# A mixture-of-experts stage on one core: token transposes two experts ahead, and down products interleaved with gate products

## What is computed

```python
dispatch = dispatch.at[flat_e, pos_c].add(tokens[tidx] * valid[:, None])
g = jnp.einsum('ech,ehi->eci', dispatch, gate_w)
u = jnp.einsum('ech,ehi->eci', dispatch, up_w)
expert_out = jnp.einsum('eci,eih->ech', jax.nn.silu(g) * u, down_w)
...
output = jnp.zeros((t, h), tokens.dtype).at[tidx].add(contrib)
```

## Time and profile before

| what | value |
|---|---|
| median of three runs | 1327.19 us (1311.12 to 1372.49) |
| the profiled execution's own time | 1307.97 us |
| its span on the core | 1306.2 us |
| PE, busy share of the span | 98% |
| DVE | 70% |
| ACT | 50% |
| POOL | 33% |

### The profile page before, as it was taken

The page is one execution under the profiler, slowest core; times in us unless marked ns, Lnnn a source line. Parts: engine busy times, 40 slices in busy tenths (PEclk is TensorE's granted clock), DMA queues, the critical chain, the costliest instruction groups (busy, mean ns, idle before and its releaser), DMA issues.

```text
span 1306.2 us, 22561 instructions
## 1 busy us (share of the span) xinstructions
PE 1280.0 (98%) x7565; PEld 1123.8 (86%) x7565; DVE 916.0 (70%) x1787; ACT 647.3 (50%) x1053; POOL 433.9 (33%) x344
## 2 busy tenths in 40 slices
PE   6999999999999999999999999999999999999995
PEld 5888888888888888888889999999999999999994
DVE  7878877777777777785656667667766766676662
ACT  4421232212322123221256777777877777777772
POOL 1000000000000000000014666777666667676653
PEclk9999999999999999999999999999999999999998
DMA  7336554664546645445447999999999999999995
GB/s 269 121 107 163 130 121 127 157 166 98 130 119 153 167 104 131 114 118 134 134 133 214 286 278 286 287 290 292 290 291 285 298 291 287 282 295 285 298 277 65
DMA packets 203800, 263.65 MB, mean 202 GB/s; under 512 B 49268, under 2 KB 138744, under 8 KB 203768
## 3 DMA queue, kind: packets, MB, share of 16 engines
q1 hardware_dynamic: 175096, 191.93, 50.9%
q0 software_dynamic: 28672, 71.32, 23.7%
HBM read 178.18 MB, written 71.39 MB: 191 GB/s over the span
## 4 chain that ended last, share of the span: by engine, by line
PE 96%; DVE 2%; DMA 1%; ACT 0%; issue 0%; POOL 0%; SPq 0%; ACTq 0%
PE pmm L1255 18%; PE pmm L1257 18%; PE pmm L1256 18%; PE pout L1255 11%; PE pout L1257 11%; PE pout L1256 11%; PE ptr L1488 4%; PE plog L1316 2%; PE plog L1325 1%; PE ptr L1267 0%; DMA out_dram<-outs,slot_cols 0%; DVE stats L829 0%; DMA xbuf<-_L_attn_proj_matrix_dram 0%; DVE xt_lo L795 0%; PE plog L1345 0%
## 5 line engine op out<-in xcount | busy, mean ns | idle before, releaser
L1614 POOL DMA_INDIRECT out_dram<-outs,slot_cols x128 | 228.7, 1787 | 165.6 <-DMA out_dram<-outs,slot_cols 136.2
L1255 PE MATMUL pmm<-xt_hi,proj_hi 128*128 128x256 f32 (+1 forms) x784 | 253.0, 323 | 2.2 <-DVE xt_lo L795 1.4
L1257 PE MATMUL pmm<-xt_hi,proj_lo 128*128 128x256 f32 (+1 forms) x784 | 249.6, 318 | 0.0
L1256 PE MATMUL pmm<-xt_lo,proj_hi 128*128 128x256 f32 (+1 forms) x784 | 249.6, 318 | 0.0
L1255 PE MATMUL pmm<-xt_hi,sgu_hi 128*128 128x256 f32 (+1 forms) x768 | 246.1, 320 | 0.2 <-issue 0.2
L1256 PE MATMUL pmm<-xt_lo,sgu_hi 128*128 128x256 f32 (+1 forms) x768 | 243.4, 317 | 0.0
L1257 PE MATMUL pmm<-xt_hi,sgu_lo 128*128 128x256 f32 (+1 forms) x768 | 243.4, 317 | 0.0
L1598 POOL TENSOR_TENSOR earlier<-earlier,chosen 128x64 bf16<-128x64 bf16 x64 | 23.9, 373 | 617.8 <-DVE chosen L916 614.0
L1604 POOL DMA_INDIRECT xbuf<-rows,slot_cols x128 | 175.3, 1369 | 80.8 <-issue 38.6
L552 ACT ACTIVATE feat<-pmm,ab 128x512 f32<-128x512 f32 x68 | 46.7, 687 | 292.4 <-PE pmm L1257 286.4
L1255 PEld LDWEIGHTS pmm<-xt_hi,proj_hi 128*128 128x128 f32 x784 | 147.3, 188 | 13.6 <-ACT feat L552 1.6
(11 more groups left out here) (185 smaller groups left out, 2543.7 us busy)
## 6 DMA issues: line engine op xcount, KB each, us to landing
raw<-in_L_ffn_gate_w_dram SPq DMA_DIRECT2D x64, 512.0 KB
raw<-in_L_ffn_up_w_dram SPq DMA_DIRECT2D x64, 512.0 KB
raw<-in_L_ffn_down_w_dram SPq DMA_DIRECT2D x64, 512.0 KB
outs<-in_L_attn_x_dram SPq DMA_DIRECT2D x32, 512.0 KB, 3.9
out_dram<-outs SPq DMA_DIRECT2D x32, 512.0 KB, 3.0
xbuf<-in_L_attn_x_dram SPq DMA_DIRECT2D x52, 256.0 KB, 7.6
raw<-xn SPq DMA_DIRECT2D x52, 256.0 KB, 6.2
rows<-raw SPq DMA_DIRECT2D x39, 256.0 KB, 4.2
```

Of the source, the lines that this page charges most:

```text
L1255: pe.matmul(psum, lh, rh, start=first and n == 0, stop=False)
L1256: pe.matmul(psum, lh, rl, start=False, stop=False)
L1257: ins = pe.matmul(psum, ll, rh, start=False, stop=final and n == len(pairs) - 1)
L1614: pool.indirect_dma_start(out=out, out_offset=bass.IndirectOffsetOnAxis(ap=slot_cols[:, at:at + 1], axis=0), in_=outs[e.b][:, c, :], in_of ...
```

## The change

Nothing of the arithmetic changes. The transposes are done one expert earlier: two experts ahead instead of one. The gate products of expert e+1 leave `e_gate_up` and are done together with the down products of expert e-1 in a new function, `e_down_gate`: one down product, two gate products, and so on, first for bank `pout[0]` and the first half of `pmm[0]`, then for the second ones. The six waits of both stand at the head of this block. The order per expert is now:

- PE: up(e), the lookup, transposes(e+2), the mixed block of down(e-1) and gate(e+1)
- ACT: `gate_up_hi`(e+1), `e_silu`(e), `down_hi`(e), `e_turned_hi`(e+2), `e_hidden_hi`(e), `e_out`(e-1), the sign sums
- DVE: `gate_up_lo`(e+1), `down_lo`(e), `e_hidden`(e), `e_turned_lo`(e+2), `e_hidden_lo`(e), the lookup's part

The diff:

```diff
--- before.py
+++ after.py
@@ -738,12 +738,12 @@
                         e_out_made, 1)
 
             def stage(e, next_rows=True, next_weights=True, out_prev=True, look=None):
-                if next_rows:
-                    e_turned_hi(e.next())
                 if next_weights:
                     gate_up_hi(e.next())
                 e_silu(e)
                 down_hi(e)
+                if next_rows:
+                    e_turned_hi(e.next().next())
                 e_hidden_hi(e)
                 if out_prev:
                     e_out(e.prev())
@@ -751,6 +751,7 @@
                     sum_signs(look)
 
             e_turned_hi(turn(0))
+            e_turned_hi(turn(1))
             stage(turn(0), next_weights=False, out_prev=False)
             for b in range(2):
                 act.wait_ge(out_stored[b], 16 * GROUPS)
@@ -759,7 +760,7 @@
                 for k in range(CHUNK):
                     stage(four(2 * m + 1, k), look=m + 2 if k == 1 else None)
             for n in range(E - 6, E - 1):
-                stage(turn(n))
+                stage(turn(n), next_rows=n < E - 2)
             stage(turn(E - 1), next_rows=False, next_weights=False)
             e_out(turn(E - 1))
 
@@ -1224,18 +1225,19 @@
                                   ALU.subtract).then_inc(e_hid_lo_made, 1)
 
             def stage(e, next_rows=True, next_weights=True, look=None):
-                if next_rows:
-                    e_turned_lo(e.next())
                 if next_weights:
                     gate_up_lo(e.next())
+                down_lo(e)
                 e_hidden(e)
-                down_lo(e)
+                if next_rows:
+                    e_turned_lo(e.next().next())
                 e_hidden_lo(e)
                 if look is not None:
                     look[0](look[1])
 
             e_turned_lo(turn(0))
             output(turn(GROUPS - 1), 3)
+            e_turned_lo(turn(1))
             stage(turn(0), next_weights=False)
             stage(turn(1))
             with dve.Fori(0, CHUNKS - 2) as m:
@@ -1502,6 +1504,31 @@
                              xt_lo[e.b][:, h, E_COLS]) for h in range(HB)])
                     ins.then_inc((e_gate_done, e_up_done)[m], 1)
 
+            def e_down_gate(d, g):
+
+                pe.wait_ge(e_hid_lo_made, d.n + 1)
+                pe.wait_ge(edn_lo_made, d.n + 1)
+                pe.wait_ge(e_xt_lo_made, g.n + 1)
+                at_least(pe, e_hid_made, g.n)
+                pe.wait_ge(egu_lo_made[0], g.n + 1)
+                for c in range(CB):
+                    at_least(pe, e_out_made, CB * (d.n - 1) + c + 1)
+                    at = slice(c * P, (c + 1) * P)
+                    cols = [slice(h * I + c * P, h * I + (c + 1) * P) for h in range(HB)]
+                    downs = [(lh[:, d.b, i, at], rh[d.b][:, i * H:(i + 1) * H]) for i in range(IB)
+                             for lh, rh in ((hid_hi, edn_hi), (hid_hi, edn_lo), (hid_lo, edn_hi))]
+                    gates = [(lh[g.b][:, cols[h]], rh[g.b][:, h, E_COLS]) for h in range(HB)
+                             for lh, rh in ((egu_hi, xt_hi), (egu_hi, xt_lo), (egu_lo, xt_hi))]
+                    for n in range(len(gates)):
+                        if n % 2 == 0:
+                            k = n // 2
+                            ins = pe.matmul(pout[c], *downs[k], start=k == 0, stop=k == len(downs) - 1)
+                            if k == len(downs) - 1:
+                                ins.then_inc(down_done, 1)
+                        gate = pe.matmul(pmm[0][:, c * CAP:(c + 1) * CAP], *gates[n], start=n == 0,
+                                         stop=n == len(gates) - 1)
+                gate.then_inc(e_gate_done, 1)
+
             def e_down(e):
                 pe.wait_ge(e_hid_lo_made, e.n + 1)
                 pe.wait_ge(edn_lo_made, e.n + 1)
@@ -1520,20 +1547,22 @@
             pe.wait_ge(out_free, 2 + J * GROUPS)
             e_turn(turn(2))
             e_gate_up(turn(1))
-            e_down(turn(0))
+            e_turn(turn(3))
+            e_down_gate(turn(0), turn(2))
             with pe.Fori(0, CHUNKS - 2) as m:
                 for k in range(CHUNK):
                     e = four(2 * m + 1, k)
-                    e_turn(e.next())
-                    e_gate_up(e)
+                    e_gate_up(e, (1,))
                     if k == 1:
                         look_up(m + 2)
-                    e_down(e.prev())
+                    e_turn(e.next().next())
+                    e_down_gate(e.prev(), e.next())
             for n in range(E - 6, E - 1):
-                e_turn(turn(n + 1))
-                e_gate_up(turn(n))
-                e_down(turn(n - 1))
-            e_gate_up(turn(E - 1))
+                e_gate_up(turn(n), (1,))
+                if n < E - 2:
+                    e_turn(turn(n + 2))
+                e_down_gate(turn(n - 1), turn(n + 1))
+            e_gate_up(turn(E - 1), (1,))
             e_down(turn(E - 2))
             e_down(turn(E - 1))
```

## The result

The changed kernel takes 1619.84 us (median of 6 runs, 1618.79 to 1620.75) against 1310.72 us before (six runs too): 1.234 times as long, 95% interval 1.228 to 1.240. The ratio is of undisturbed executions; the kernel before shows now and then a slower one at a lower clock, such as 1372.49 us. The forecast was 1505 us with a range up to 1580 us. The direction was right and the size was not: between the profiled executions (1307.97 and 1618.79 us) 311 us were added where 197 us were forecast.

What follows compares the result with a forecast made beforehand. It took PE to bound the kernel before, and a chain of waits through ACT and DVE after; 154 us of chain, 31 of lookups and a later start (187 us) on 1308 gave 1495, plus 10 for the clock: 1505 us, range 1465 to 1580.

Steps and rivals of the forecast that it cites:

- The waits that close a loop: Mixed block waits for hid, hid behind down_lo and ACT's down_hi, that behind e_out: 11.8 us per expert against 9.27.
- Rival (a): PE stays the bound and gains only what mixing gives, 0 to 29 us: 1279 to 1308 us; chance 0.05.
- the one that mixing costs 1.2 us per block: Rival: pauses before down products in the mixed block add 74 us, 1579 us in total; chance 0.06.
- The length of the chain at full clock: From one mixed block's start to the next: 11.8 us, or 14.5 us where ACT does the sign sums.
- The terms for chain, lookups and start: 154 us for 61 intervals, 31 us for 14 lookups, about 1.6 us for the later first block: together 187 us.
- DVE to PE: Hand-over from the end of hid to the mixed block's first product: 0.06 us, the chain's last link.
- The clock: PE's clock was seen to fall 4 to 5 us into an idle time; some 4.7 us lookup stalls would bring half speed.
- for a third of the 14: Clock falls behind the 14 long lookup stalls, 2.2 us of work lost each, counted for a third: 10 us.
- a granted clock under 0.9: Sign that the prediction is wrong, if seen on PE over a normal expert stage.
- Rival (b): Clock falls in every stall, 2.2 us of work lost per expert, 134 us more, about 1630 us; chance 0.07.
- Mixing: Products in the mixed block keep their spacings of before, 0.118 us for gate and 0.229 us for down.
- The queues counted at nothing: SP's weight refills and POOL's gathers cost nothing, since the longer stage covers them.

Runs made afterwards that it cites:

- e1: Changed kernel with hid made ahead of down_lo on DVE, nothing else: 1453.54 us, 1.110 times the kernel before.
- e3: Changed kernel with all 12 down products ahead of the 24 gate products, not interleaved: 1379.57 us, 1.054 times the kernel before.
- e6: Changed kernel with only a lookup's sign sums moved ahead of e_out on ACT: 1568.01 us, 1.196 times the kernel before.
- e11: Changed kernel with PE's wait for hid at the mixed block's head replaced by a wait for silu: 1358.71 us, 1.037 times the kernel before.
- e7: Changed kernel with useless products before PE's wait for hid, 20 in the stage behind a lookup, 9 in others: 1504.70 us, 1.148 times the kernel before.
- e4: Changed kernel with silu between ACT's two conversions, sign sums ahead of e_out, and hid between DVE's two low parts: 1347.78 us (1.029).
- e8: e4 with down products first, waits for hid, tokens and gate weights behind them, slot numbers one stage earlier: 1342.82 us (1.024).
- e2: Changed kernel with useless products before PE's wait for hid, 20 in the lookup's own stage, 9 in others: 1555.22 us, 1.188 times the kernel before.

## Why the prediction was right and wrong

**The waits that close a loop: right.** e1, e3, e6 and e11 each cut one link and took off 166, 240, 52 and 261 us. Each came within 5 us of, or inside, what the chain gave for it. Rival (a), that PE stays the bound, is out, and so is the one that mixing costs 1.2 us per block.

**The length of the chain at full clock: right within 10%.** The terms for chain, lookups and start gave 187 us. e7, with the clock held up and a hand-over to PE as short as in the prediction, has 195.5 us, and its blocks follow each other by 11.8 to 12.0 us, or 14.5 us with the sums, against 11.8 and 14.5 us in the forecast. With the hand-over of the changed kernel it is about 206 us. Of the single links in the rows above, the conversions took 2.08 us (2.06 in the prediction), silu to down_hi 0.48, down_lo to hid 1.14, hid 0.68. One was off: DVE to PE took 0.36 us, 1485.54 + 0.68 to 1486.58, where the prediction took 0.06 us from a place with one wait. The trace shows where it goes: the wait for hid is the first of three steps that PE's sequencer makes one after another, at 1486.26, 1486.37 and 1486.47, before the block's first weight load at 1486.57. Before 1472.95 there is one such step and the hand-over takes 0.19 us; in e7 the weight load itself waits for hid, and it takes 0.05 us. All together this is the 10 us by which e7's hand-overs are shorter.

**The clock: wrong, and this is the step that failed.** The sum counted it "for a third of the 14", 10 us, and let the short stalls go free because the one fall that was seen came 4 to 5 us into an idle time. Measured: 61 half-speed stretches for 61 stalls (60 in the window above and one at 1585.7 us), 256 us at half clock, about 105 us of cost where 10 us were counted. The 46 stalls of 2.0 to 2.6 us were all followed by one. The prediction had named a granted clock under 0.9 as a sign that it was wrong, and it was 0.85. Rival (b), with 0.07 for its chance, was what happened. Its price of 2.2 us of work per stall gave 1630 us, 10 us too much. The price is half of an estimated 4.4 us that stands in none of the rows it names; the runs show 105 / 61 = 1.7 us. That (b) came so near in the total is in part luck: its clock term was 30 us too large, and the chain 19 us too short.

The error in the argument was to read a threshold for a single idle time from one fall at the end of the program. Between the blocks the idle time returns every 12 us. And the loss does not fall on work that has slack: it falls on the mixed block's first half, which leads to the last down product and so is a link of the chain. From the block's first product to e_out it took 7.22 us (1472.95 to 1480.17) instead of 5.65 us. The longer period then carries the same idle time at the same place.

The Trainium skill ("TensorE: Matmul & The Clock Gate", HAM oscillation) describes this loop for a kernel that waits for transfers between bursts of products: each burst begins at the low clock. The trace agrees, with a wait for another engine in the transfers' place, in the 14 stalls of 5.1 us, in which the clock fell while PE still stood. In the other 47 the block began at full clock, and it fell 0.03 to 1.2 us later (1472.95 and 1474.1 above).

**Mixing: right to within its size.** The spacings of before were taken over; it costs 0.085 us per expert. The isolated spacing of the Trainium skill ("TensorE: Matmul & The Clock Gate", Back-to-back issue gap, 0.109 and 0.216 us) is not reached by mixing: 0.117 and 0.2375 us.

**The queues counted at nothing: half wrong.** The cover I named, the longer stage, was there in the changed kernel, where PE never waited for rows. With the chain cut the cover is gone, and the gathers were late by up to 2.2 us in one expert of four (e4, e8), because POOL's gather stands behind adds that wait for e_out. That is the cost of transposing two experts ahead without moving POOL.

## What to carry to other kernels

When a piece of work is moved to an engine's critical place, write down what it waits for and follow that wait around every engine until it comes back to the same place; if the loop's sum is longer than the bound engine's work, the loop is the new period, however idle the engines in it look. Wait for the last reader of a buffer and not for something that comes after it, and put last in a stage what nobody waits for. An idle time that returns each period has to be charged twice, once as itself and once as the clock it may cost, above all where the work behind it is in the loop; to tell the two apart, fill it with useless products, and look whether the filler changed another link as well. Of several waits at one place, each may cost a step behind the one that ends last: here 0.1 us each.

## What was not expected

Useless work made the kernel faster: e7 issues 712 useless products and takes 115 us less, of which about 105 because the granted clock goes from 0.85 to 1.00 over the expert stage.

The idle time after which the clock fell depends on more than its length. At 2.0 to 2.6 us per stage it fell each time in the changed kernel. At 2.5 to 2.6 us once in four experts it fell 8 times in 14 (e3), at 2.9 us 11 times (e2), at 3.8 us 13 times (e1). At 1.4 to 2.2 us it fell 4 times in 14 (e8), and at 0.7 to 1.2 us in e1 never. In e11 two short stalls, of 0.6 to 1.3 and 0.9 to 1.5 us, stand about 2 us apart in one stage of four, and there it fell 4 times in 14. What decides it is not shown by these runs.
